# A vision tower on one core: two stages overlapped at their seam, and one of two transposes handed from TensorE to a DMA

## The reference

```python
h = tok(x, W, b)                       # patch embedding
h = concatenate([cls_tok, h], axis=1)  # 64 x 197 x 192
h = h + attn(layernorm(h), ...)        # 12 heads of 64, 4-bit fake quantisation at every step
h = h + ffn(layernorm(h), ...)

def bitlinear(x, w, g):
    x_norm = rmsnorm(x, g)
    x_q = activation_quant(x_norm)     # 8-bit: round(x * 127 / max|x| of the row)
    w_q = weight_quant(w)              # ternary
    return x_q @ w_q.T
def ffn(x):
    up, gate = split(bitlinear(x, w_in, g_in))      # 192 -> 2 x 512
    y = silu(gate) * up
    return bitlinear(y, w_out, g_out)               # 512 -> 192
```

## Time and profile before

| what | value |
|---|---|
| median of 3 runs | 1281.3 us (1279.3 to 1283.15) |
| profiled execution: its time | 1279.7 us |
| profiled execution: span from first to last instruction | 1277.7 us |
| PE / DVE / ACT / POOL busy, share of the span | 86% / 85% / 73% / 36% |
| mean granted TensorE clock | 0.893 of full speed |

### The profile page before, as it was taken

How to read it: one execution, slowest core, us unless ns; L and a number is a source line. 1 busy time by engine, 2 the same in 40 slices (tenths; PEclk the granted TensorE clock), 3 DMA queues, 4 the chain that set the end, 5 groups by cost and what they waited for, 6 DMA issues and landing times.

```text
span 1277.7 us, 31970 instructions
## 1 busy us (share of the span) xinstructions
PE 1098.7 (86%) x10782; PEld 678.1 (53%) x10782; DVE 1086.9 (85%) x1979; ACT 933.1 (73%) x1877; POOL 462.4 (36%) x540
## 2 busy tenths in 40 slices
PE   7999995799999999999999999996367577777776
PEld 6999995245555555555555555554233344444443
DVE  6666777189999999999999999999479989899886
ACT  0000000699999999999999999995178888888886
POOL 5544434002211222211112221112256666666664
PEclk9999998699999999999999999998566867777776
DMA  8999994136655655555555665555212322223222
GB/s 284 313 282 294 292 308 161 44 129 161 160 144 142 141 147 159 159 145 141 145 147 160 152 146 142 148 147 143 52 53 82 93 82 84 86 82 90 86 75 73
DMA packets 158358, 187.63 MB, mean 147 GB/s; under 512 B 42864, under 2 KB 119744, under 8 KB 158016
## 3 DMA queue, kind: packets, MB, share of 16 engines
q1 hardware_dynamic: 90656, 138.99, 34.3%
q10 hardware_dynamic: 52224, 37.37, 9.5%
q0 software_dynamic: 15360, 9.70, 8.0%
HBM read 143.06 MB, written 36.12 MB: 140 GB/s over the span
## 4 chain that ended last, share of the span: by engine, by line
PE 71%; ACT 9%; issue 7%; DVE 6%; DMA 3%; POOL 2%; ACTq 1%; SPq 0%; DVEq 0%; POOLq 0%
PE psum L1066 13%; PE psum L1131 12%; PE psum L1194 11%; PE psum L1164 7%; PE psum L1134 7%; PE psum L1227 6%; PE psum L1147 6%; PE psum L1181 5%; ACT yi L608 2%; ACT big L601 2%; ACT ysq L628 2%; DVE big L1041 1%; PE psum L1248 1%; ACT zi L616 1%; PE psum L1082 1%
## 5 line engine op out<-in xcount | busy, mean ns | idle before, releaser
L917 DVE TENSOR_TENSOR pi<-big 128x2364 int16<-128x2364 f32 (+1 forms) x128 | 333.2, 2603 | 11.4 <-DMA big<-z_row 11.3
L707 POOL DMA_DIRECT2D h_res<-att x128 | 135.3, 1153 | 563.7 <-ACT att L545 554.5
L569 ACT ACTIVATE big<-psum 128x788 f32<-128x788 f32 (+1 forms) x384 | 330.3, 862 | 0.4 <-DVE pi L917 0.3
L531 ACT ACTIVATE qki<-psum 128x394 int16<-128x394 f32 x384 | 172.5, 509 | 17.4 <-PE psum L1134 5.6
L1066 PE MATMUL psum<-big 128*128 128x192 f32 (+1 forms) x1128 | 182.5, 326 | 1.5 <-DMA big<-xt 1.5
L1066 PEld LDWEIGHTS psum<-big 128*128 128x128 f32 (+1 forms) x1128 | 180.6, 188 | 2.6 <-issue 1.8
L1227 PE MATMUL psum<-winb,zT 96*128 96x512 bf16 (+1 forms) x396 | 146.9, 538 | 31.1 <-DVE big L1041 30.2
L1194 PE MATMUL psum<-big,sa_hot 128*32 128x197 f32 (+1 forms) x3072 | 168.9, 337 | 0.6 <-DVE zt L941 0.6
L531 ACT ACT_TABLE_LOAD x1 | 1.3, 1283 | 226.6 <-PE psum L1134 226.6
L741 POOL TENSOR_TENSOR big<-big,goutb 128x512 f32<-128x512 f32 (+1 forms) x99 | 123.8, 1271 | 80.3 <-DVE big L1041 80.3
L1131 PE MATMUL psum<-xT,w1b 128*128 128x394 bf16 x384 | 108.3, 342 | 25.2 <-DMA xT<-x_int 16.2
(11 more groups left out here) (105 smaller groups left out, 1826.2 us busy)
## 6 DMA issues: line engine op xcount, KB each, us to landing
big<-z_row SPq DMA_DIRECT2D x192, 394.0 KB, 5.0
big<-xt SPq DMA_DIRECT2D x98, 384.0 KB, 4.6
tin<-h_res SPq DMA_DIRECT2D x49, 192.0 KB, 2.4
tres<-h_res ACTq DMA_DIRECT2D x49, 192.0 KB, 2.5
out<-oo ACTq DMA_DIRECT2D x49, 192.0 KB, 2.6
h_res<-big ACTq DMA_DIRECT2D x78, 96.0 KB, 4.4
h_res<-att POOLq DMA_DIRECT2D x64, 96.0 KB, 3.1
x_int<-big ACTq DMA_DIRECT2D x93, 64.0 KB, 4.2
```

Source lines behind the costliest of these rows:

```text
L531: act.activation(qki[:, k, :, :], psum[:, bank, 0:2 * N] .rearrange("p (c n) -> p c n", c=2), ACT.Copy, scale=factor[(F_Q, F_K)[b % 2]])\
L569: act.activation(ex[0:r, tri, t, 4 * g:4 * g + 4, :].rearrange("p (a h) n -> p a h n", a=2), psum[0:r, 2 * t:2 * t + 2, 0:2 * N] .rearrang ...
L707: pool.dma_start(h_res[bass.ds(b - 4, 1), t0:t0 + r, :].rearrange("a n d -> (a n) d"), att[0:r, par, t, :], accum_op=ALU.add).then_inc(s_a ...
L917: v.tensor_tensor(pi[0:r, t, :, 0:N], ex[0:r, it, t, :, :], zb[0:r, ip, :, :], ALU.mult).then_inc(s_pi, 1)
```

## The change

Three things change together.

**The passage.** The pair steps 0 to 3 are now placed between the last image steps, at a place of its own on every engine (`EARLY = 4`), and the loads wait only for the images whose tokens they read (`wait_added`). SP loads the input of pair t+1 in step t, so the first load is issued behind SP's last image step.

**The order in a step.** On PE the transposes of x now stand ahead of the input matmuls. On DVE the statistics are joined before the largest value of `yg`, the dequantising factors (`factors(4)`) are made before y instead of behind it, and the largest value of x is taken last. Those factors now lie in a tile of their own with four places, `ft` ("ring of four"), since they live longer.

**The transposes of y.** PE's 8 transposes and ACT's copy out of PSUM are gone. SP issues one DMA transpose from `yi3` to `yTi` (128 partitions x 1024 int16) in step t+4, and DVE converts that to bf16, `yT3`, two steps later. The back of the pipeline is one step longer (`LAGS` 7 to 8): output matmuls, result and store move from pair t-5 and t-6 to t-6 and t-7.

The core of the diff:

```diff
 SP
-            for p in range(2):
-                sp.wait_ge(s_added[p], 32 * (B // 2))
-            def pair_step(t, par):
-                if at := pair_of(t)(0):
-                    wait_apart(sp, s_t["zc"], t - 1)
-                    sp.dma_start(tin[0:r, par, 0:n, :], pair_rows(h_att, t, r, n)).then_inc(s_t3[par], 16)
+            def pair_step(t, par, q):
+                if at := pair(-1):
+                    if isinstance(t, int):
+                        wait_added(sp, t + 1)
+                    wait_apart(sp, s_t["zc"], t)
+                    sp.dma_start(tin[0:r, oth, 0:n, :], pair_rows(h_att, t + 1, r, n)).then_inc(s_t3[oth], 16)
+                if at := pair(4):
+                    wait_apart(sp, s_t["yi"], t - 3)
+                    wait_apart(sp, s_t["yT_read"], t - 5)
+                    sp.dma_start_transpose(yTi[:, par, 0:4 * n, 0:r], yi3[0:r, par, 0:n, :].rearrange("p a h -> p (a h)"))\
+                      .then_inc(s_ym[par], 16)
 ACT
-                if at := pair(5):
-                    act.wait_ge(s_t["yT_summed"], t - 4)
-                    act.activation(yT3[:, 0:n, :, 0:r], psum[:, 5, :].bitcast(i16) ..., ACT.Copy).then_inc(s_t["yT_read"], 1)
+            images(image_step, -2, B + 2)
+            pairs(pair_step, 0, 1)
+            images(image_step, B + 3, B + 3)
+            pairs(pair_step, 2, EARLY - 1)
+            images(image_step, B + 4, B + 4)
             over_pairs(act, pair_step)
 POOL
+            images(image_step, -2, B + 1)
+            pairs(pair_step, 0, 1)
+            images(image_step, B + 2, B + 2)
+            pairs(pair_step, 2, EARLY - 1)
+            images(image_step, B + 3, B + 3)
 DVE
+                if at := pair(6):
+                    dve.wait_ge(s_ym[par], loads_of(t - 6, par))
+                    wait(dve, s_t["o_summed"], t - 6)
+                    v.tensor_copy(yT3[:, 0:n, :, 0:r], yTi[:, par, 0:4 * n, 0:r] ...).then_inc(s_t["yT_read"], 1)
...
-                if at := pair(3):
-                    dve.wait_ge(s_t["y"], 2 * (t - 3) + at[1])
-                factors(4)
+            images(image_step, -2, B + 2)        # pair step 0 inside image step B + 1, ahead of normalise
+            pairs(pair_step, 1, 2)
+            images(image_step, B + 3, B + 3)
+            pairs(pair_step, 3, EARLY - 1)
 PE
+            images(image_step, -2, B + 2)
+            pairs(pair_step, 0, 1)
+            images(image_step, B + 3, B + 3)
+            pairs(pair_step, 2, EARLY - 1)
+            images(image_step, B + 4, B + 4)
+        def wait_added(eng, t):
+            last = (256 * (t + 1) - 1) // N if t < 8 else B - 1
+            for p in range(2):
+                wait(eng, s_added[p], 32 * ((last - p) // 2 + 1))
```

More of the change, by code:

```diff
@@ L312, in vit_tower_kernel @@
         zi3 = sb("zi3", [128, 2, 2, D], i16)
+        yTi = big[:, o_pt + n_pt:o_pt + n_pt + 1024].bitcast(i16).rearrange("p (i k n) -> p i k n", i=2, k=8)
         zT3 = sb("zT3", [KH, 2, 2, 2, 128], bf16)
@@ L324, in vit_tower_kernel @@
         wdeq4 = sb("wdeq4", [128, 2, 2], fp32)
-        MS, RMS, MAX, T_, A127, INV, S_, F_ = range(8)
+        ft = sb("ft", [128, 4, 2, 2], fp32)
+        MS, RMS, MAX, T_, A127, INV, S_ = range(7)
         def val(which, par, k, rows, n=None):
@@ L339, in over_pairs @@
         def over_pairs(eng, step):
-            first = (LAGS + 3) // 2 * 2
-            for t in range(first):
-                step(t, t % 2)
+            first = 14
+            for t in range(EARLY, first):
+                step(t, t % 2, t % 4)
             whole = (NPAIR - 1 - first) // UNROLL * UNROLL
@@ L346, in over_pairs @@
                 for j in range(UNROLL):
-                    step(UNROLL * i + first + j, j % 2)
+                    step(UNROLL * i + first + j, j % 2, (first + j) % 4)
             for t in range(first + whole, NPAIR + LAGS):
-                step(t, t % 2)
+                step(t, t % 2, t % 4)
         def pair_rows(dram, j, rows, n):
@@ L357, in loads_of, with images, pairs @@
             return 16 * ((j - par) // 2 + 1) if isinstance(j, int) else 8 * (j - par) + 16
-        def over_images(eng, step):
-            for b in range(-2, B + 5):
-                step(b, b % 2, b % 3)
+        EARLY = 4
+        def images(image_step, first, last):
+            for b in range(first, last + 1):
+                image_step(b, b % 2, b % 3)
+        def pairs(pair_step, first, last):
+            for t in range(first, last + 1):
+                pair_step(t, t % 2, t % 4)
+        def wait_added(eng, t):
+            last = (256 * (t + 1) - 1) // N if t < 8 else B - 1
+            for p in range(2):
+                wait(eng, s_added[p], 32 * ((last - p) // 2 + 1))
         def dst_rows(dram, y, x, half, along_x):
@@ L605, in pair_step @@
                     act.wait_ge(s_t["factors"], t)
-                    wait(act, s_t["yT_summed"], t - 5)
+                    if not isinstance(t, int) or t > 5:
+                        act.wait_ge(s_ym[par], loads_of(t - 6, par))
                     for a in range(n):
@@ L1211, in image_step, with pair_step @@
                         scores(b, par, u)
-            over_images(pe, image_step)
-            pe.wait_ge(evac["y"], B)
-            def pair_step(t, par):
+            def pair_step(t, par, q):
                 pair, oth = pair_of(t), 1 - par
+                if at := pair(2):
+                    r, n = at
+                    pe.wait_ge(s_t["xi"], t - 1)
+                    wait(pe, s_t["xT_read"], t - 2)
+                    dst = psum[0:KH, 4, :].bitcast(bf16)[:, 0:512].rearrange("p (a c n) -> p a c n", a=2, c=2)
+                    for a in range(n):
+                        for c in range(2):
+                            last = nc.tensor.transpose(dst[:, a, c, 0:r], zi3[0:r, par, a, c * KH:(c + 1) * KH].bitcast(bf16),
+                                                       ident[0:r, 0:r])
+                    last.then_inc(s_t["xT_summed"], 1)
                 if at := pair(3):
```

255 lines of the change are left out of this document (119 added, 136 removed).

## The result

| kernel | median of the runs | ratio to before, 95% interval |
|---|---|---|
| before | 1280.36 us (1279.30 to 1283.15) | |
| changed | 1259.89 us (1257.96 to 1262.34) | 0.9838 [0.9811, 0.9865] |

What follows compares the result with a forecast made beforehand. DVE was taken as fullest, 6.13 of 6.83 us a step, alternating with a low-clock loop through PE. 918 + 4 x 7.07 + 45 x 6.4 + 13 = 1247 us span, so 1250 us; range 1237 to 1260.

Steps and rivals of the forecast that it cites:

- signs of being wrong: DVE waiting for yi or `tin`, clock at 0.6 or below with silu waiting for input matmuls, last images over 5 us later.
- The passage: At the seam: pair steps among the last images bring the first y from 931.95 to about 918 us, 14 us earlier.
- The tail: From last y to end of span: 10.9 us before, 2 us added for DMA and copy, 13 us.
- The dequantising factors: On DVE, made ahead of y: 0.15 instead of 0.69 us, a gain of 0.54 us a step.
- The new copy: On DVE, int16 to bf16, 1024 elements: 0.54 us from similar clips, upper bound 1.22 us.
- The DMA transpose: On SP: lands about 5 us after issue, hidden up to 6.5 us at a step of 6.4 us.
- The step that failed: Feed-forward step time: 6.2 to 6.6 us depending on how low and upper clock mix, taken as 6.4 against 6.83.
- the loop: zi, transposes of x, input matmuls, second silu, yi, zi: 7.07 us at the low clock, 5.13 at the upper.
- the fill: Start of the feed-forward pipeline after the first y: four steps at the low clock, 4 x 7.07 us.
- the low clock binds: Rival, 17%: with less PE work the low clock sets steps of 6.83 to 7.07 us; 1278, or 1268 us.
- The argument against it: Against the low-clock rival: 5.7 us of PE work in a 7.07 us low-clock step exceeds the present 72% share.
- DVE: Fullest engine in the feed-forward steps: 6.13 us busy a step before, 6.2 us after, its waits for POOL gone.

Runs made afterwards that it cites:

- run a: Changed kernel with the passage undone: all image steps before pair step 0 on every engine; 1269.5 us, 0.992 of before.
- run m: run c with the dequantising factors made behind y again, after the wait for y to be complete; 1256.4 us, 0.983 of before.
- i: Changed kernel with every DMA transpose of y issued twice, the first time into a tile nobody reads; 1260.4 us, 0.987 of before.
- run c: Changed kernel with zi ahead of yi in ACT's step; 1236.3 us, 0.967 of before.
- j: Kernel before with one edit, the transposes of x ahead of the input matmuls on PE; 1374.5 us, 1.076 of before.
- b: Changed kernel with the transposes of x behind the input matmuls again on PE; 1242.5 us, 0.972 of before.

## Why the prediction was nearly right, by its own steps

The time of 1259.9 us lies within the stated range, 1237 to 1260, by 0.1 us. That is luck: the upper end was for a clock near 0.75 with steps of 6.6 us, and the time was reached with steps of 6.69 us at the low clock. One of the prediction's own signs of being wrong came true in full, a granted clock below 0.6 with silu waiting for the input matmuls. Two more came true at the seam, and no wait from 960 to 1230 us follows from them: DVE waited 3.54 us for its first `tin` (2.57 us at this place before, for the broadcast), and the last image ended 10 us later instead of at most 5.

- **The passage** came out as worked: transposes of x at 912.4 (about 912), first y at 917.75 (about 918); in run a, undoing it brings the first y back to 927.35. But it was credited with all 14 us; by run a and its fill, about 3 of them are the order inside the step.
- **The tail**: 13.6 us, forecast 13.
- **The dequantising factors**: 0.13 us instead of 0.69, as forecast; run m shows the gain in place, 0.42 of the 0.54 us.
- **The new copy**: 0.42 us, forecast 0.54 from the clips, bound 1.22.
- **The DMA transpose**: landed in 3.1 us, forecast 5, with 6.5 allowed; shown to be hidden by i. The Trainium skill's figure of 1309 ns for one 128x128 block ("VectorE: DVE Perf Modes", "The three transpose paths"), added up over eight blocks, is an estimate of 10.5 us. The trace does not agree: it has all eight in 3.1 us, fixed cost included.
- **The step that failed** is the last one of the sum: "if low and upper clock mix inside each step ... I take 6.4". It rests on a granted clock that stays near 0.75. The clock fell to 0.50 for 204 us and to 0.54 in the mean, so the loop, rightly seen and priced at 7.07 (6.77 in fact), bound nearly everywhere: 49 x (6.69 - 6.4) = 14 us, of which the fill's 2.7 us for four low-clock steps come off. This was the rival "the low clock binds", which had 17%, at 1268 if the step just stayed (1269 by its own terms); its mechanism came true, at 6.69 for the step instead of 6.83 to 7.07. The argument against it, that PE would be busy for more of a low-clock step than it had been on average, did not hold: it was 79% busy there (160.6 of 204 us; 72% before) and the clock stayed down.
- **DVE** did not set the step. It was 89% busy, with its 0.7 us of idle time as before. The 6.2 us worked out for it is what it reached in run c, 6.21, where the loop was open.

Why the clock stays low with this pattern of work and rises with 0.9 us more of it stays open: the runs show that it is so for transposes and for matmuls, not by what rule.

## What to carry to other kernels

When work is taken off an engine whose clock depends on its work, price the step at the low clock first, and ask which loop through the other engines that clock would close; here moving two blocks of ACT's list (zi ahead of yi) opened it and was worth more, 24 us, than the whole change. Order inside one engine's list can be judged only together with the lists that wait for it: x first on PE cost 95 us where ACT's copy, ahead of silu, waits for transposes of the same step (j), and 17 us where that copy is gone (b against the changed kernel). The fastest version found is run c, 1236.3 us, 3.3% faster than before.

## What the runs showed of the hardware that was not expected

- Dead work on PE made the kernel faster: 8 transposes a step lifted the clock from 0.54 to 0.82 and saved 12.7 us; 2 matmuls of 512 columns, 0.54 to 0.72 and 8.3 us.
- SP's issue of the transpose from SBUF, 1024 blocks of 256 bytes, took 1.25 us, hardly more than the 1.21 us for the transpose of 448 packets from DRAM in the attention.
- A small DVE instruction that waits for y, the large one just before it, to be complete takes 0.69 us (L990 before, L958 in run m); the same four elements take 0.13 us where other instructions stand between (L958 in the changed kernel). What the 0.56 us are made of, no run shows.
